# An attention kernel's opening rewritten: x ahead of the tables, normalised on ScalarE, six projection banks, a written-out unit 0

## The reference

```
xn = (x - mean) / sqrt(var + 1e-5)
q, k, v = xn @ wq.T, xn @ wk.T, xn @ wv.T       # 32 query heads, 8 key/value heads of 128
q, k = rope(q), rope(k)
p = softmax(q k^T / sqrt(128) * key_scale + causal)
s = (p v) @ wo.T
g = silu(sum over 4 experts of top-2 gate * (xn A_e^T) B_e^T * 4)
out = x + s * g
```

## Time and profile before

| | |
|---|---|
| median of 3 runs | 1355.3 us |
| lowest, highest | 1354.82, 1359.77 us |
| the profiled execution's own time | 1357.92 us |
| its span, first to last instruction | 1356.1 us |
| PE busy | 1322.2 us, 98% of the span |
| DVE, ACT, POOL busy | 969.6, 961.8, 423.0 us |
| mean granted clock of TensorE | 0.990 of full speed |

### The profile page before, as it was taken

The page is one execution under the profiler, slowest core; times in us unless marked ns, Lnnn a source line. Parts: engine busy times, 40 slices in busy tenths (PEclk is TensorE's granted clock), DMA queues, the critical chain, the costliest instruction groups (busy, mean ns, idle before and its releaser), DMA issues.

```text
span 1356.1 us, 22594 instructions
## 1 busy us (share of the span) xinstructions
PE 1322.2 (98%) x6982; PEld 1106.6 (82%) x6982; DVE 969.6 (72%) x2449; ACT 961.8 (71%) x2513; POOL 423.0 (31%) x341
## 2 busy tenths in 40 slices
PE   7599999999999999999999999999999999999997
PEld 5588888788888888888888888888888888888885
DVE  6786678667766777776776777677777767777775
ACT  3586668777777777687776768777676877777773
POOL 4332321403314142143323224141331433223321
PEclk9699999999999999999999999999999999999998
DMA  6000000201100000010000000000000100012223
GB/s 217 16 17 5 24 24 9 62 17 47 47 24 32 0 23 23 0 31 15 23 8 15 15 15 31 0 31 0 23 23 0 31 15 23 8 31 85 73 80 119
DMA packets 23385, 43.64 MB, mean 32 GB/s; under 512 B 2480, under 2 KB 2608, under 8 KB 23344
## 3 DMA queue, kind: packets, MB, share of 16 engines
q1 hardware_dynamic: 20592, 37.76, 9.0%
q10 hardware_dynamic: 2752, 5.38, 1.1%
HBM read 34.74 MB, written 8.39 MB: 32 GB/s over the span
## 4 chain that ended last, share of the span: by engine, by line
PE 93%; DVE 4%; ACT 1%; issue 1%; DMA 1%; POOL 0%; SPq 0%; ACTq 0%; DVEq 0%
PE bank_a L461 19%; PE bank_b L461 18%; PE bank_b L555 13%; PE o_ps L555 12%; PE pv_ps L548 10%; PE pair L532 7%; PE pair L539 6%; PE pair L528 2%; PE pair L530 1%; PE bank_a L518 1%; PE o_ps L461 1%; DVE x_sb L975 1%; PE o_ps L508 1%; DMA x_sb<-x 1%; DVE pT_lo L1117 0%
## 5 line engine op out<-in xcount | busy, mean ns | idle before, releaser
L376 POOL TENSOR_TENSOR rot<-rot,tab 128x512 f32<-128x512 f32 x160 | 208.3, 1304 | 603.2 <-ACT rot L777 602.9
L820 ACT ACTIVATE probs<-probs,row_min 128x128 f32<-128x128 f32 (+1 forms) x512 | 225.5, 447 | 0.0
L839 ACT ACTIVATE pT_hi<-pair 128x768 fp32r<-128x768 f32 x128 | 104.0, 812 | 170.9 <-PE pair L539 170.2
L831 ACT ACTIVATE probs<-probs,row_inv 128x128 f32<-128x128 f32 (+1 forms) x512 | 190.8, 446 | 26.7 <-DVE row_inv L1147 26.4
L1117 DVE TENSOR_TENSOR pT_lo<-pair,pT_hi 128x768 fp32r<-128x768 f32 x128 | 121.7, 950 | 92.6 <-ACT pT_hi L839 92.3
L361 POOL TENSOR_TENSOR w_hi<-raw,zero 128x512 fp32r<-128x512 f32 x74 | 84.8, 1147 | 247.6 <-PE bank_a L461 131.2
L461 PE MATMUL bank_b<-xT_hi,w_hi 128*128 (+1 forms) x380 | 153.3, 403 | 2.8 <-DVE xT_lo L988 2.8
L461 PE MATMUL bank_a<-xT_hi,w_hi 128*128 (+1 forms) x380 | 154.8, 408 | 0.5 <-DVE xT_lo L988 0.4
L1097 DVE TENSOR_TENSOR q_lo<-cosx,q_hi 128x512 fp32r<-128x512 f32 x128 | 118.2, 924 | 47.1 <-ACT q_hi L784 46.9
L461 PE MATMUL bank_b<-xT_hi,w_lo 128*128 (+1 forms) x380 | 149.5, 393 | 0.0
L461 PE MATMUL bank_b<-xT_lo,w_hi 128*128 (+1 forms) x380 | 149.1, 392 | 0.0
(11 more groups left out here) (166 smaller groups left out, 3237.6 us busy)
## 6 DMA issues: line engine op xcount, KB each, us to landing
raw<-w_seq SPq DMA_DIRECT2D x76, 256.0 KB, 2.6
gate_scratch<-b_raw ACTq DMA_DIRECT2D x16, 256.0 KB, 2.0
out<-y_sum SPq DMA_DIRECT2D x16, 256.0 KB, 2.0
x_sb<-x SPq DMA_DIRECT2D x3, 1024.0 KB, 12.6
mid<-x SPq DMA_DIRECT2D x8, 256.0 KB, 2.7
mid<-gate_scratch SPq DMA_DIRECT2D x8, 256.0 KB, 2.9
raw<-x SPq DMA_DIRECT2D x7, 256.0 KB, 2.7
raw<-gate_scratch SPq DMA_DIRECT2D x7, 256.0 KB, 2.9
```

The source lines that it names most:

```text
L376: nc.gpsimd.tensor_tensor(v, v, tab[:, s:s + SEQ].unsqueeze(1).to_broadcast([P, 2, SEQ]), ALU.mult).then_inc(sin_done[kind], 1)
L820: a = nc.scalar.activation(s, s, ACT.Exp, bias=row_min[:, j % 2, i:i + 1], scale=-1.0, accum_out=row_sum[:, i:i + 1])
L831: a = nc.scalar.activation(s, s, ACT.Copy, scale=row_inv[:, i:i + 1])
L839: nc.scalar.activation(pT_hi[:, :, :], pair[j % 2][:, :, 0:ROWS], ACT.Copy).then_inc(pThi_done, 1)
```

## The change

- SP's queue: block 0 of x, then the weight tiles of K and H0, then the tables without the identity, then the other four weight tiles, blocks 1 to 3 and b_raw. ACT's queue loads only the identity, with a semaphore of its own (ident_in), for which PE waits instead of the tables; the first users of the tables wait for tables_in themselves.
- Normalising goes from DVE (subtract, multiply) to ACT: DVE makes shift = -mean * rstd (shifts), ACT runs Identity with scale rstd and bias shift in place (x_shifted), for all 16 tiles.
- In the first unit V and H3 are projected into the two halves of pair[1]; x tiles 4 to 7 are transposed into the halves of pair[0]; v is transposed into pv_ps.
- keep_clock uses the 128 columns of the identity alone, 20 such matmuls in all.
- ACT, DVE and POOL have a written-out order for the opening and unit 0 (act_opening, dve_opening, pool_opening), which replaces the opening and act_unit(0), dve_unit(0) and the first round of POOL's group(0, 1). PE's pe_unit(0) keeps its order; its opening is changed as below. From unit 1 on nothing is changed.

```diff
-        first_banks = [pair[0][:, 0, :], pair[0][:, 1, :], pair[1][:, 0, :], pair[1][:, 1, :],
-                       pair[1][:, 0, :], pair[1][:, 1, :], pv_ps[:, :], o_ps[:, :]]
+        first_banks = [pair[0][:, 0, :], pair[0][:, 1, :], pair[1][:, 0, :], pair[1][:, 1, :]] + \
+                      [pair[0][:, 0, :], pair[0][:, 1, :]] * 2
+        FIRST_V, FIRST_H3 = pair[1][:, 0, :], pair[1][:, 1, :]
+        FIRST = (WK, WQ, WQ + 1, WQ + 2, WV, WQ + 3)
...
             for t in range(BLOCK_TILES):
                 sp.dma_start(x_sb[:, t, :], x_t[t, :, :]).then_inc(x0_in[t], 16)
-            for c in range(len(landing)):
+            for c in range(WQ + 1):
+                sp.dma_start(landing[c], w_seq[c, :, :]).then_inc(land_in[c], 16)
+            sp.dma_start(tab[:, 0:T_IDENT], tables[:, 0:T_IDENT]).then_inc(tables_in, 16)
+            for c in range(WQ + 1, len(landing)):
                 sp.dma_start(landing[c], w_seq[c, :, :]).then_inc(land_in[c], 16)
...
+            for half in range(2):
+                sp.dma_start(b_raw[ER * half:ER * (half + 1), :], b_t).then_inc(b_in, 16)
...
-            pe.wait_ge(tables_in, 16)
-
-            def keep_clock(columns, times):
+            pe.wait_ge(ident_in, 16)
+
+            def keep_clock(times):
                 for _ in range(times):
-                    nc.tensor.matmul(o_ps[:, 0:columns], ident, tab[:, 0:columns], start=True, stop=True)
-
-            keep_clock(512, 2)
+                    nc.tensor.matmul(o_ps[:, 0:P], ident, ident, start=True, stop=True)
+
+            keep_clock(8)
             for t in range(BLOCK_TILES):
                 turn_x(t, first_banks[t])
-                keep_clock(P, 2)
-            keep_clock(512, 1)
+                keep_clock(2)
+            keep_clock(4)
...
             project(H2, o_ps, WQ + 2, 0, 1)
-            bank_free(K, 1)
-            project(V, bank_a, WV, 0, 1)
             turn_x(4, first_banks[4])
             turn_x(5, first_banks[5])
-            bank_free(H0, 1)
-            project(H3, bank_b, WQ + 3, 0, 1)
+            project(V, FIRST_V, WV, 0, 1)
+            pe.wait_ge(xlo_done, 5)
+            turn_x(6, first_banks[6])
+            pe.wait_ge(xlo_done, 6)
+            turn_x(7, first_banks[7])
+            project(H3, FIRST_H3, WQ + 3, 0, 1)
+            pe.wait_ge(vT_done, 1)
+            bank_free(H1, 1)
+            turn_v(pv_ps)
+            pe.wait_ge(xlo_done, X_FIRST)
             for kind in (K, H0, H1):
                 pe.wait_ge(q_ready[kind], 1)
             scores(0)
-            bank_free(H1, 1)
-            turn_x(6, first_banks[6])
-            bank_free(H2, 1)
-            turn_x(7, first_banks[7])
-            pe.wait_ge(vT_done, 1)
-            turn_v()
-            pe.wait_ge(xlo_done, X_FIRST)
+            bank_free(H0, 1)
+            project(H0, bank_b, WQ, BLOCK, 1)
+            bank_free(K, 1)
+            project(K, bank_a, WK, BLOCK, 1)
             bank_free(H3, 1)
-            project(H0, bank_b, WQ, BLOCK, 1)
             for kind in (H2, H3):
                 pe.wait_ge(q_ready[kind], 1)
             scores(1)
-            pe.wait_ge(v_ready, 1)
-            project(K, bank_a, WK, BLOCK, 1)
...
+        def x_shifted(t0, t1, count):
+
+            nc.scalar.wait_ge(shift_done, count)
+            for t in range(t0, t1):
+                nc.scalar.activation(x_sb[:, t, :], x_sb[:, t, :], ACT.Identity, bias=shift[:, t:t + 1],
+                                     scale=rstd[:, t:t + 1]).then_inc(norm_done, 1)
...
-            nc.scalar.dma_start(tab[:, :], tables).then_inc(tables_in, 16)
-            for half in range(2):
-                nc.scalar.dma_start(b_raw[ER * half:ER * (half + 1), :], b_t).then_inc(b_in, 16)
...
+            nc.scalar.dma_start(ident, tables[:, T_IDENT:T_COLS]).then_inc(ident_in, 16)
...
-        def normalise(tiles, count):
+        def shifts(t0, t1, count):
             nc.vector.wait_ge(rstd_done, count)
-            for t in tiles:
-                nc.vector.tensor_scalar(x_sb[:, t, :], x_sb[:, t, :], meanvar[:, t, 0:1], rstd[:, t:t + 1],
-                                        ALU.subtract, ALU.mult).then_inc(norm_done, 1)
+            nc.vector.scalar_tensor_tensor(out=shift[:, t0:t1], in0=meanvar[:, t0:t1, 0], scalar=-1.0,
+                                           in1=rstd[:, t0:t1], op0=ALU.mult, op1=ALU.mult).then_inc(shift_done, 1)
```

Of the written-out orders, the piece on DVE from the first probabilities to the low part of item 0:

```diff
+            row_inverse(1)
+            block_statistics(3)
+            mask_rows(1, 2)
+            rows_low(0, 1)
+            v_low(1, pv_ps)
```

More of the change, by code:

```diff
@@ L797, in copy_vT, with v_high @@
                 act.wait_ge(vt_ps, before_count)
-            nc.scalar.activation(v_T[:, :], bank_a[:, :], ACT.Copy).then_inc(vT_done, 1)
-        def v_high(count, used):
+            nc.scalar.activation(v_T[:, :], bank[:, :], ACT.Copy).then_inc(vT_done, 1)
+        def v_high(count, used, bank=bank_a):
             act = nc.scalar
@@ L909, in _ @@
         @block.scalar
         def _(act):
-            nc.scalar.dma_start(tab[:, :], tables).then_inc(tables_in, 16)
-            for half in range(2):
-                nc.scalar.dma_start(b_raw[ER * half:ER * (half + 1), :], b_t).then_inc(b_in, 16)
-            def first_high(c):
-                nc.scalar.wait_ge(land_in[c], 16)
-                nc.scalar.activation(w_hi[:, c, :], landing[c], ACT.Copy).then_inc(whi_done, 1)
-            for t in range(BLOCK_TILES - 1):
-                x_high(t, first_banks[t])
@@ L921, in _ @@
-            first_high(WK)
-            x_high(BLOCK_TILES - 1, first_banks[BLOCK_TILES - 1])
-            for c in range(WQ, WQ + 3):
-                first_high(c)
-            swap_halves(K, bank_a, 1, None, None)
-            first_high(WV)
-            swap_halves(H0, bank_b, 1, None, None)
-            first_high(WQ + 3)
-            k_high(1, None)
-            swap_halves(H1, pv_ps, 1, H0, 1)
-            q_high(H0, 1, None)
-            swap_halves(H2, o_ps, 1, K, 1)
-            q_high(H1, 1, None)
@@ L934, in _ @@
-            copy_vT(1, None)
-            x_high(4, first_banks[4])
-            x_high(5, first_banks[5])
-            swap_halves(H3, bank_b, 1, H1, 1)
-            act.wait_ge(w_ready[WQ + 2], 1)
-            act.wait_ge(w_ready[WQ + 3], 1)
-            act.wait_ge(w_ready[WV], 1)
-            low_scores(0, 1)
-            q_high(H2, 1, None)
-            x_high(6, first_banks[6])
-            x_high(7, first_banks[7])
-            v_high(1, None)
-            q_high(H3, 1, None)
-            exponents(0, 1)
@@ L948, in _ @@
-            swap_halves(H0, bank_b, 2, H3, 1)
-            low_scores(1, 2)
-            normalise_rows(0, 1)
-            swap_halves(K, bank_a, 2, H2, 1)
-            exponents(1, 2)
-            for u in range(WRITTEN):
+            nc.scalar.dma_start(ident, tables[:, T_IDENT:T_COLS]).then_inc(ident_in, 16)
+            act_opening()
+            for u in range(1, WRITTEN):
                 act_unit(u)
@@ L1249, in dve_unit, with dve_opening @@
                 row_inverse(n4[6])
[L1251 to L1260 removed]
+        def dve_opening():
+            first_statistics(0)
+            first_statistics(1)
+            first_statistics(2)
+            shifts(0, 1, 1)
+            shifts(1, 2, 2)
+            first_statistics(3)
+            shifts(2, 3, 3)
+            shifts(3, 4, 4)
+            x_low(0, first_banks[0])
+            x_low(1, first_banks[1])
+            x_low(2, first_banks[2])
+            x_low(3, first_banks[3])
             block_statistics(1)
[L1262 removed]
+            block_statistics(2)
+            shifts(4, 8, 5)
             cos_product(K, bank_a, 1)
[L1264 removed]
             cos_product(H0, bank_b, 1)
+            rotate(H0, 1)
             rotate(K, 1)
[L1267 to L1268 removed]
             q_low(H0, 1)
@@ L1290, in _ @@
-            cos_product(K, bank_a, 2, H2, 1)
             rotate(K, 2)
-            row_inverse(2)
-            for u in range(WRITTEN):
+            attn_low(0, 1)
+            shifts(12, 16, 7)
+            q_low(H0, 2)
+            rows_low(1, 2)
+            mask_rows(2, 3)
+            dve_side(0, 1, 0)
+            cos_product(H1, bank_a, 2, H0, 2)
+            rotate(H1, 2)
+            row_inverse(3)
+            dve_side(0, 1, 1)
+            mask_rows(3, 4)
+            k_low(2)
+            q_low(H1, 2)
@@ new lines, in dve_opening @@
+            dve_side(0, 1, 2)
+            cos_product(H2, bank_b, 2)
+            dve_side(0, 1, 3)
+            attn_low(1, 2)
+            rows_low(2, 3)
+            rotate(H2, 2)
+            dve_side(0, 2, 0)
+            row_inverse(4)
+            cos_product(H3, bank_b, 2, H1, 2)
+            dve_side(0, 2, 1)
+            attn_low(2, 3)
+            rotate(H3, 2)
+            mask_rows(0, 5)
+            q_low(H3, 2)
+            q_low(H2, 2)
+            rows_low(3, 4)
+            cos_product(H0, bank_b, 3, H3, 2)
@@ L1294, in _ @@
+            cos_product(K, bank_a, 3, H2, 2)
+            row_inverse(5)
```

(12 more changed lines are left out.)

208 lines of the change are left out of this document (147 added, 61 removed).

## The result

| | before | after |
|---|---|---|
| median of the runs compared, us | 1356.24 (4 runs, 1354.82 to 1359.77) | 1342.43 (4 runs, 1342.1 to 1343.54) |
| profiled execution, us | 1357.92 | 1342.1 |
| its span, us | 1356.1 | 1340.3 |

The ratio is 0.9898, with a 95% interval of 0.9882 to 0.9913: faster by 1.0%. The forecast was 1342.0, range 1338 to 1348. In four later batches of runs the kernel before had medians of 1357.37 (13 runs), 1357.27 (19), 1358.12 (7) and 1357.53 (9), so the 1355.3 from which the forecast subtracted was about 2 us low. The change is worth nearer to 15 us than to 13.3. That the median came out within 0.4 us of the forecast is in part luck, as two errors of about 2 us cancel.

A forecast was written before the change was run, and what follows sets the result against it. PE was taken to bound the kernel, with its losses in the opening. Start 14.45, work 64.7, stops 6.0 and half clock 2.3 gave 87.4 instead of 100.7; 1355.3 less 13.3 made 1342.0, range 1338 to 1348.

The forecast's parts named there:

- work: PE's work from the first projection to unit 0's last output matmul: 64.7 us, kept by the change.
- Start of the first projection: Opening: with x landing at about 3.4 and ACT normalising, PE starts at 14.45 instead of 15.91, 1.5 us gained.
- Six banks and the stop before scores(0): Opening: V and H3 in pair[1] and no 5.74 us normalising on DVE remove 6.4 us of PE stops.
- From scores(0) to scores(2): Unit 0's first scores: PE stops 1.0, then 3.7 us with handovers, where 7.7 stood before; rows ready at 46.1.
- Unit 0: Rest of unit 0: a stop of 1.0 us at x_low(8) and one of 0.3 for x_low(10).
- The clock: Before scores(2): one fall of PE's clock is left, costing 2.3 instead of 5.3 us, 3.0 gained.
- Rival 1: Opening: the clock falls before the first projection too, 1.7 us likely, 1343.7, with later handovers 1345; chance 0.20.
- Rivals 2 and 4: Before scores(2): stop too short for clock to fall, 1339.7, chance 0.13; or 7.7 us stop stays, 1349 to 1351, 0.05.
- Rival 3: Opening: ACT is the bound, at 1.2 us a tile rather than 0.73, 6 us more, 1348; chance 0.10.
- Rival 5: Opening: slower through the two-operand ACT pass; gain gone at 1.75 us a tile, 1358.6 at 2.0; chance 0.02.
- Behind that point the program is the same: After unit 0's last output matmul, the program was claimed to be unchanged.
- The base: The median of three runs before, 1355.3 us, from which the forecast subtracted 13.3; the profiled execution took 1357.92.

The follow-up runs named there:

- Experiment 1: The changed kernel with the old order of loads (all tables and b_raw on ACT's queue from the start): 1345.1 us, 2.7 more than after.
- Experiment 2: The changed kernel with V and H3 of the first unit projected into bank_a and bank_b again: 1342.7 us, 0.3 more than after.
- experiment 3: The changed kernel with normalising back on DVE (subtract and multiply) and none of it on ACT: 1347.77 us, 5.3 more than after.
- experiment 9: The changed kernel with normalise_rows(1) moved ahead of low_scores(2) on ScalarE, no added matmuls: 1341.91 us, against 1342.74 for after in the same batch.
- Experiments 8 and 11: After plus 14 identity matmuls before scores(2), normalise_rows(1) ahead of low_scores(2): 1340.42 us (8); also ACT passes over tiles 12 to 15 one by one: 1341.6 (11).
- experiment 4: The changed kernel with each of the 16 ACT passes over x made twice: 1356.07 us, 13.6 more than after.
- Experiment 12: After plus 14 identity matmuls before scores(2), normalise_rows(1) ahead of low_scores(2), EPS added by a two-tensor operation: 1347.83 us, on another chip.

## Why the prediction was right, point by point

Against the split of the prediction, all to the last output head of unit 0: start 14.03 (forecast 14.45), work 63.9 (64.7), stops 5.3 (6.0), half clock 2.4 (2.3); sum 85.7 (87.4). The work is what remains of 85.68 - 14.03 when stops and half clock are taken off.

- **Start of the first projection**: right. Landing 3.59 (3.4), ScalarE's tile 0.80 with a spacing of 0.71 (0.82 and 0.73). The estimate from a per-row operand's 0.11 us held for this pass. Experiment 1 shows that this part needs the early x: without it, the start is later than before.
- **"Six banks and the stop before scores(0)"**: size right, 6.4 us of stops are gone, but the step credited two causes and only one acts. Experiment 2 gives the banks 0.3 us, which the runs can't tell from nothing; experiment 3 puts the work back on DVE and 3.0 us of stops return. Nor was the 5.74 us of DVE's pass a price of having it on DVE: with the new order it takes 1.91 there. The other 3.4 us belong to the new order, in parts that no run separates.
- **From scores(0) to scores(2)**: right in the times, not in the path. The forecast had scores(2) at 46.1 and stops of 1.0 and 3.7; measured 46.10, 0.9 and 3.5. Block 3's statistics end at 42.97 and the mask starts at 43.31 with 0.33 of wait: the margin of 0.4 was real. But the forecast led to the exponents over H3's swap, sine product, sum and mask_rows(0), which end at 37.61, and left block 2's four ACT passes out of this sum. They run until 37.51, q_high(H3) follows, and the exponents start behind it at 37.93 (the row at 34.69 in the chain). The two paths differ by 0.3 us, so the number came out.
- **Unit 0**: 1.0 forecast, 0.9 measured at one tile; the second, of 0.3, did not come.
- **The clock**: one fall in 44 to 53, as written. Rival 1, a fall ahead of the first projection, did not come: 14 to 40 us is at 1.00 in after and in its repeat. PE stood 0.6 us ahead of it in after; in experiment 9 it stood 1.9 us there, and the clock from 14 to 30 us was 1.00 as well.
- **Rivals 2 and 4** did not come: the clock fell behind the stop of 3.5 us, and that stop is not the 7.7 of before.
- **Rival 3, ScalarE as the bound**: its price did not come (0.71 us a tile, not 1.2), but its engine is on the chain of after already, with block 2's tiles and the work behind them from 34.3 to 43.3 us. Experiments 8 and 11 show it further on: what is gained behind scores(2) is waited for later, at a result that hangs on ScalarE.
- **Rival 5, the slower one**: its price per tile was wrong. The prediction let a tile cost what it takes, 13 times, and put the point of decision at 1.75 us a tile; experiment 4, with 1.3 us left of the gain, puts it just above 1.42. What the step left out is that longer stops let the clock fall, 4 us of the 13.6.
- **"Behind that point the program is the same"**: it took 0.8 us less than in before (1254.6 against 1255.4). Experiment 12 shows that the same order of instructions is not the same time there.
- **The base**: the median of 3 runs, 1355.3, was 2 us under that of the later batches. The sum for the profiled execution, 1344.6, missed by 2.5; the median by 0.4.

## What to carry to other kernels

When an engine's queue holds a long pass ahead of small results that TensorE waits for, try the pass on an engine that stands idle at that moment, even if it is slower there by half; here the queue position decided, and the rate per operation did not. Judge a stop by when its awaited result starts, not by how long the stop is, and count the half clock behind a long stop as part of its price. Check a freed resource such as a bank on its own before you credit it.
